# A four-layer network on one core: transposes one pair ahead in the mixing stage, and a memory attention with negated, pre-scaled scores

## What is computed

```python
x = x + tanh(g_ffn[1])   * mixing(_layernorm(x))               # layer 1, feed-forward
x = x + tanh(g_xattn[2]) * memory_attention(_layernorm(x), ctx, mask)   # layer 2, attention

def mixing(x):                      # eight 256x256 factors, summed beforehand
    return einsum('btd,rde->bte', x, factors) / sqrt(8) + bias

def memory_attention(h, m, mask):
    scores = einsum('bsd,bmd->bsm', h, m) / sqrt(256)
    scores = where(mask, scores, -1e30)
    attn = softmax(scores)          # over the 128 memory rows
    out = einsum('bsm,bmd->bsd', attn, m)
    return where(any(mask), out, 0)
```

## Time and profile before

| | |
|---|---|
| median of three timed runs | 903.51 us (902.8 to 904.79) |
| the profiled execution, its own time | 905.36 us |
| its span, first to last instruction | 903.5 us |
| busy: PE / DVE / ACT / POOL | 762.5 / 589.0 / 420.9 / 341.4 us |
| chain that ended last, by engine | PE 53%, DVE 14%, SPq 9%, ACT 8%, issue 8%, POOL 5%, DMA 3% |
| mean granted TensorE clock | 0.909 of full speed |

### The profile page before, as it was taken

How to read it: one execution, slowest core, us unless ns; L and a number is a source line. 1 busy time by engine, 2 the same in 40 slices (tenths; PEclk the granted TensorE clock), 3 DMA queues, 4 the chain that set the end, 5 groups by cost and what they waited for, 6 DMA issues and landing times.

```text
span 903.5 us, 16057 instructions
## 1 busy us (share of the span) xinstructions
PE 762.5 (84%) x4547; PEld 503.1 (56%) x4555; DVE 589.0 (65%) x1388; ACT 420.9 (47%) x920; POOL 341.4 (38%) x571
## 2 busy tenths in 40 slices
PE   3999896998684289898999968999997889999982
PEld 2455454555342156595788756566666555666641
DVE  5799696778776966874322382688874865444446
ACT  3566464676571013341377557666662233333320
POOL 5000552455347613337367652000020761333320
PEclk9999897999997597957999989899997799999995
DMA  6354309999008890144445362000004222232226
GB/s 207 121 175 126 99 9 301 310 287 312 22 0 323 304 283 1 42 183 143 143 147 152 105 195 86 20 20 21 12 1 140 94 95 77 84 87 86 66 79 215
DMA packets 90507, 116.86 MB, mean 129 GB/s; under 512 B 12421, under 2 KB 81064, under 8 KB 89146
## 3 DMA queue, kind: packets, MB, share of 16 engines
q1 hardware_dynamic: 83658, 99.01, 36.2%
q0 software_dynamic: 6768, 16.86, 5.2%
HBM read 54.90 MB, written 58.43 MB: 125 GB/s over the span
## 4 chain that ended last, share of the span: by engine, by line
PE 53%; DVE 14%; SPq 9%; issue 8%; ACT 8%; POOL 5%; DMA 3%; DVEq 0%; POOLq 0%; ACTq 0%
PE ps L2195 8%; SPq L398 7%; PE ps L2086 5%; PE ps L1770 5%; PE ps L2217 4%; POOL x_rows L601 3%; PE ps L1760 3%; PE ps L2104 3%; ACT work L824 2%; ACT probs_t L830 2%; PE ps L1966 2%; PE ps L2079 2%; PE ps L1806 2%; PE ps L2162 2%; PE ps L2069 2%
## 5 line engine op out<-in xcount | busy, mean ns | idle before, releaser
L830 ACT ACTIVATE probs_t<-ps 128x1024 f32<-128x1024 f32 x64 | 65.6, 1024 | 72.8 <-PE ps L1770 72.8
L1223 DVE TENSOR_REDUCE row_max<-ps 128x8 f32<-128x1024 f32 x64 | 77.5, 1210 | 12.0 <-PE ps L1760 11.8
L1087 ACT ACTIVATE ctx_cols<-ctx_cols 128x256 f32<-128x256 f32 x54 | 22.5, 417 | 124.0 <-DVE ctx_cols L1619 124.0
L1229 DVE TENSOR_TENSOR work<-ps,row_max 128x1024 f32<-128x1024 f32 x64 | 76.9, 1202 | 1.2
L1619 DVE TENSOR_TENSOR ctx_cols<-ps,ctx_rows 128x512 f32<-128x512 f32 x54 | 37.3, 690 | 60.6 <-PE ps L2195 60.5
L1770 PE MATMUL ps<-ident,work 128*128 128x128 f32 x512 | 70.6, 282 | 3.3 <-ACT work L824 2.1
L2195 PE MATMUL ps<-early,xt 128*128 x152 | 71.5, 593 | 0.0
L2217 PE MATMUL ps<-early,ctx_cols 128*128 (+1 forms) x216 | 57.7, 391 | 12.2 <-ACT ctx_cols L1092 12.2
L1770 PEld LDWEIGHTS ps<-ident,work 128*128 128x128 f32 x512 | 57.2, 143 | 18.7 <-ACT work L824 13.2
L642 POOL DMA_INDIRECT y_rows<-ctx_cols,w2d x38 | 37.5, 988 | 78.7 <-DMA y_rows<-ctx_cols,w2d 49.0
L2217 PEld LDWEIGHTS ps<-early,ctx_cols 128*128 128x128 f32 x216 | 41.7, 195 | 41.5 <-issue 23.2
(11 more groups left out here) (328 smaller groups left out, 1895.7 us busy)
## 6 DMA issues: line engine op xcount, KB each, us to landing
x_rows<-pad_row SPq DMA_DIRECT2D x1, 17415.0 KB, 68.5
work<-x_rows SPq DMA_DIRECT2D x77, 129.0 KB, 2.1
x_rows<-pad_row SPq DMA_DIRECT2D x1, 7740.0 KB, 36.0
x_rows<-pad_row SPq DMA_DIRECT2D x1, 7611.0 KB, 93.7
early<-in_w3st SPq DMA_DIRECT2D x8, 512.0 KB, 6.4
work<-y_rows SPq DMA_DIRECT2D x16, 256.0 KB, 2.9
early<-y_rows SPq DMA_DIRECT2D x8, 512.0 KB, 7.4
late<-in_w2u SPq DMA_DIRECT2D x1, 2304.0 KB, 8.7
```

What stands on the lines that cost most here:

```text
L830: act.activation(probs_t[:, :, :], ps[:, 4:6, :], ACT.Copy).then_inc(sem("att.evac"), 1)
L1223: dve.tensor_reduce(row_max[:, u, 8 * c:8 * c + 8], scores(c), AX.X, ALU.max).then_inc(sem("att.max"), 1)
L1229: dve.tensor_tensor(probs[:, u, c, :].rearrange("p (h k) -> p h k", k=P), scores(c), row_max[:, u, 8 * c:8 * c + 8].unsqueeze(2).to_broadc ...
```

## The change

Two edits, independent of each other in the code.

**Mixing.** PE now transposes pair t+2 ahead of the products of pair t (`turn_mix`, `mixing`), the first two pairs before any product. ACT's copies alternate between the two pairs of slots of `xt4`, and its wait for `main3` moves two tiles back. DVE normalises two pairs ahead of the first product and from then on pair t+4 instead of t+2. The hardware loops of the stage are written out on PE and ACT.

**Memory attention.** ACT's copy of the transposed tiles multiplies by -1/16, the mask row has the other sign, so the scores arrive negated and scaled; DVE takes their minimum, which is the bias of the exponential as it stands (its scale is then -1). The two 128x1 products and their semaphores go.

```diff
-            def front_ring(L):
-                def body(t, first, last):
-                    for u in range(2):
-                        act.wait_ge(sem("front.tr"), FRONT[L] + t + u + 1)
-                        wait(act, sem(f"main{L}"), t + u - 1)
-                        act.activation(xt[:, u], bank(TP + u, D).rearrange("p (j n) -> p j n", j=2),
-                                       ACT.Copy).then_inc(sem("front.out"), 1)
-                return body
-
-            tile_pairs(act, front_ring(3))
+            for k in range(NT // 2):
+                for u in range(2):
+                    act.wait_ge(sem("front.tr"), FRONT[3] + 2 * k + u + 1)
+                    wait(act, sem("main3"), 2 * k + u - 3)
+                    act.activation(xt4[k % 2][:, u], bank(TP + u, D).rearrange("p (j n) -> p j n", j=2),
+                                   ACT.Copy).then_inc(sem("front.out"), 1)
...
-                    act.wait_ge(sem("l2.bias"), 2 * k + u + 1)
+                    act.wait_ge(sem("l2.least"), 2 * k + u + 1)
...
-                    act.activation(p_l2[:, u], bank(u, P), ACT.Exp, scale=D ** -0.5, bias=sc_l2[:, u, 1:2],
+                    act.activation(p_l2[:, u], bank(u, P), ACT.Exp, scale=-1.0, bias=sc_l2[:, u, 1:2],
...
-                                   ACT.Copy).then_inc(sem("front.out"), 1)
+                                   ACT.Copy, scale=-(D ** -0.5)).then_inc(sem("front.out"), 1)
...
-                    dve.tensor_scalar(mask_bf, mask_u8[0:1], -1.0, -NEG, ALU.add, ALU.mult).then_inc(sem("mask.add"), 1)
+                    dve.tensor_scalar(mask_bf, mask_u8[0:1], -1.0, NEG, ALU.add, ALU.mult).then_inc(sem("mask.add"), 1)
...
             norm_x(3, 0)
-
-            def mixing(t, first, last):
-                if not last:
-                    norm_x(3, t + 2)
+            norm_x(3, 2)
+            for t in range(0, NT, 2):
+                if t + 4 < NT:
+                    norm_x(3, t + 4)
                 for u in range(2):
                     dve.wait_ge(sem("main3"), t + u + 1)
                     add_gated(3, t + u, bank(4 + u, D), tg[:, 5:6])
...
-            def maxima_l2(k):
+            def minima_l2(k):
                 for u in range(2):
                     dve.wait_ge(sem("main4"), 2 * k + u + 1)
-                    dve.tensor_reduce(sc_l2[:, u, 0:1], bank(u, P), AX.X, ALU.max).then_inc(sem("l2.max"), 1)
-                for u in range(2):
-                    dve.wait_ge(sem("l2.max"), 2 * k + u + 1)
-                    dve.tensor_scalar(sc_l2[:, u, 1:2], sc_l2[:, u, 0:1], -(D ** -0.5), None, ALU.mult
-                                      ).then_inc(sem("l2.bias"), 1)
+                    dve.tensor_reduce(sc_l2[:, u, 1:2], bank(u, P), AX.X, ALU.min).then_inc(sem("l2.least"), 1)
...
-            def mixing(t, first, last):
+            def turn_mix(t):
                 for u in range(2):
                     front(3, t + u, u, lambda u: pe.wait_ge(sem("qf.y"), NT))
+
+            def mixing(t):
                 for u in range(2):
                     pe.wait_ge(sem("front.out"), FRONT[3] + t + u + 1)
                     wait(pe, sem("resid3"), t + u - 1)
                     mm(bank(4 + u, D), ones3[32:35, :], b_mix, start=True, stop=False)
                     for j in range(2):
-                        op = mm(bank(4 + u, D), xt[:, u, j, :], w_mix[:, j, :], start=False, stop=(j == 1))
+                        op = mm(bank(4 + u, D), xt4[t // 2 % 2][:, u, j, :], w_mix[:, j, :], start=False, stop=(j == 1))
                     op.then_inc(sem("main3"), 1)
-            tile_pairs(pe, mixing)
+
+            turn_mix(0)
+            for t in range(0, NT, 2):
+                if t + 2 < NT:
+                    turn_mix(t + 2)
+                mixing(t)
```

More of the change, by code:

```diff
@@ L1427, in mixing @@
                     add_gated(3, t + u, bank(4 + u, D), tg[:, 5:6])
-                if last:
+                if t + 2 == NT:
                     norm_x(4, 0)
                 tile_stats(4, t, sem("resid3"))
-            for t in range(0, NT, 2):
-                mixing(t, t == 0, t == NT - 2)
             def weights_l2(k):
@@ L1465, in _ @@
                 if 1 <= k <= NT // 2:
-                    maxima_l2(k - 1)
+                    minima_l2(k - 1)
                 if k >= 2:
```

## The result

The changed kernel takes 897.9 us, the median of 13 runs (896.55 to 901.96); the kernel before, run beside it, 903.76 (901.82 to 905.98). The ratio is 0.9938, with a 95% interval of 0.9923 to 0.9954: 0.6% faster, 5.6 us by the ratio and 5.9 by the medians. The prediction said 898.6.

What follows compares the result with a forecast made beforehand. The prediction took PE to bound the mixing and DVE the memory attention's full-clock steps. Gains of 3.3 + 1.6 = 4.9 us from 903.5 gave 898.6 us, range 894.8 to 901.9, the forecast's own bounds being 897.2 to 900.3.

Steps and rivals of the forecast that it cites:

- Mixing, 3.3 us (2.4 to 3.8): Forecast gain in the mixing stage from transposing a pair ahead: 3.3 us, bounds 2.4 to 3.8.
- six groups stay between products: 6 x 0.44: Mixing: six groups of four transposes still cost 0.44 us each between products, 2.64 us together.
- The start cost: Mixing start: the second pair's transposes ahead of the first product make it 1.0 us later.
- the 0.5 that was to come back: Mixing start: the delayed first pair's last 1.0 us of work falls into the full clock, returning 0.5 us.
- the 3.8 of the upper end: Mixing at best: 4.30 us gone, less 1.0 for the later start, plus 0.5 back, gives 3.8 us.
- rival 1: Mixing: DVE becomes the bound or PE waits for normalised rows; pair 3.2 us, kernel 901.4 us; chance 0.13.
- rival 2: Mixing: the clock rises one pair later, costing 2.1 us more, kernel 900.7 us; chance 0.05.
- Memory attention, 1.6 us (0.8 to 2.5): Forecast gain in the memory attention, mainly from dropping DVE's scalings: 1.6 us, bounds 0.8 to 2.5.
- The step of 3.45: Memory attention at full clock: DVE's step of 3.65 us loses 0.20 and becomes 3.45.
- the 0.3 us by which PE's turn was to start earlier: Memory attention's low-clock opening: PE's turn starts about 0.3 us earlier because the first exponential is freed sooner; 0 to 0.5.
- rival 3: Memory attention's opening: the clock does not fall, 3.3 us less, kernel 895.3 us; chance 0.12.
- Rivals 4 and 5: 4: attention's low clock lasts longer, 2.75 us per step, chance 0.05; 5: gain lost behind the router, 901.1 us, chance 0.05.

Runs made afterwards that it cites:

- e4: The change plus nine unused 256-column products on PE ahead of the mixing stage, on the second chip; 948.02 us against 950.46 before, ratio 0.9982.
- e1: The kernel before with only the mixing edit, on the second chip; 947.81 us against 950.46, ratio 0.9987.
- e3: The kernel before plus unused filler products in PE's gaps ahead of the memory attention's first two transposes, second chip; 948.49 us against 950.46, ratio 0.9993.
- e2: The kernel before with only the memory attention edit, on the second chip; 949.48 us against 950.46, ratio 0.9983.

## Why the prediction was right, and where its sum was not

**Bound of the two stages.** As predicted: PE in the mixing (no releaser ahead of the bias), DVE in the attention's full-clock steps. These are shown, and so is what each edit does by itself; the total came out right partly by luck, as the sum below says.

**Mixing, 3.3 us (2.4 to 3.8).** At a like clock it gives 2.76 (mixing alone), 2.62 (e4) and 2.64 (the change again): within the bounds, 0.5 to 0.7 less than taken. Three terms were mis-sized, and the largest is "six groups stay between products: 6 x 0.44". The 0.44 was read where transposes follow transposes; from transposes to a bias row it is 0.53 (328.56 to 329.09), so 6 x 0.09 = 0.54 is missing. The start cost 1.16 and not 1.0, since all four of the second pair's transposes (1.05 us, 315.96 to 317.01) stood behind the wait for its rows, and not two of them. And of the 0.5 that was to come back only 0.15 to 0.29 did: the first pair's products take 4.35, 4.23 and 4.37 us in these three traces (314.82 to 319.17 in the change again) instead of 4.52, about 0.3 too little. From the 3.8 of the upper end, 3.8 - 0.54 - 0.16 - 0.3 = 2.8, against the 2.62 to 2.76 measured. The 0.5 took for granted that the clock rises at a fixed moment "whatever stands there". It rose 5.7 to 5.8 us after the first transposes in the kernel before and with the attention edit alone, but 7.1 in the filler kernel, whose start is the same code, and 6.3 to 6.5 in the three traces named. So the moment moves by itself; whether the edit moves it too is not shown. In the profiled run of after none of the 0.5 came back.

**DVE's room (rival 1).** It was enough: a pair of 2.97 has DVE wait for 0.18 us. The rival's 3.2 did not come.

**The clock in the mixing (rival 2).** This happened in the profiled run of after, a rise at 323.9 with the first pair's products all at the low clock, and not in the change run again (319.0) nor in e1 and e4 (321.4, 321.6). So it is not the order of the code that decides, but the run (or the chip: the late one is the only trace of the change on the first). Its price was put at 2.1, for a whole pair at the low clock; between two traces of the same kernel the rise is 2.7 us later, counted from the first bias, and costs 1.24, about half of that. The Trainium skill, TensorE: Matmul & The Clock Gate, Part 4: PE-mode transpose, cited for this rival, says that a transpose doesn't count as busy for the clock in the same way as other work. As far as these traces go they don't contradict it: the four more transposes at the start brought no earlier rise, which came 3.9 to 4.2 us after the first bias in four traces of that start (6.9 in after) and 4.5 to 4.7 where only one group stood ahead of it (5.9 in e3). With 5.9 in one trace of the old start the difference is no proof. If it is real, it is worth about 0.3 us here, and not the pair that the rival made of it.

**Memory attention, 1.6 us (0.8 to 2.5).** With the fall it gives 1.37 (e2) and 1.36 (the change again), without it 36.09 - 34.49 = 1.60 (the filler kernel against after, which differ in the two filled gaps too). The step of 3.45 is 3.44, and the 0.3 us by which PE's turn was to start earlier in the low-clock opening is 1.15 - 0.86 = 0.29.

**The fall (rival 3).** It was given 0.12 and a price of 3.3; the price measured is 3.36 and 3.60. The reason against it, that the gap of 0.92 stays, was right as far as it went: the gap stayed, and the clock held all the same. What was wrong was to take the fall as a fixed answer to the gap. Over the ten traces, six have both gaps unfilled and in five of them the clock fell; four have them filled or bridged, and it fell in none of those. If the gaps made no difference, all five falls would land among the six unfilled traces about once in 40 times (6 of the 252 ways to place five falls in ten traces). So the traces together speak for the gaps as what makes the fall possible. The filler's single trace can't show it, since the change held the clock once with its gaps open. What decides it within one kernel was not found. The two edits are not enough to prevent the fall: the clock fell with each alone, and in two of three traces with both.

**The sum.** At a like clock the edits give 67.97 - 63.97 = 4.0 us where 4.9 was forecast. In the trace of after comes 3.6 from the fall that stayed away, less 1.24 from the late rise: 4.0 + 3.6 - 1.24 = 6.36. That this is the table's sum is no check, since the two prices are differences of the same cuts. The 5.6 to 5.9 us of the runs is thus more than the two edits' own work explains. Ten of the 13 runs of after have a mean clock of 0.911 to 0.917 and take 896.6 to 898.2 us, the three others 0.898 to 0.900 and 899.5 to 902.0, so that the clock goes with some 4 us in the time of one kernel. It is more than the one fall: 0.013 of 897 us is 23 us more at half speed, where a fall lasts 10, and only one of these runs has a trace. One fall of 10.2 us at half speed would take the traced run's 0.913 to about 0.907 (an estimate), and no run lies between 0.900 and 0.911, so in most runs of after the fall seems to have stayed away. How often it comes in the kernel before on the first chip stays open, with one trace, and so does whether the change makes it rarer there. So the forecast was off by only 0.7 us by luck: the edits' work, sized 0.9 us too high, was made up for by a clock event that it had given 0.12. On the third chip, where the trace shows the fall, the ratio 0.9953 is 4.5 us, which is the edits' own 4.0 with little added.

**Rivals 4 and 5.** Neither came in the first pair of traces: no step of the attention is slow in after, and the rise behind the router moved by 6.4 us with the work. That a gain does not reach the end did happen on the second chip, in another way than rival 5 told (the last section).

## What to carry to other kernels

Where a stage's transposes wait for a copy, turning the next pair ahead of the products removes the wait for little: here 2.6 to 2.8 us of 28.5. Look at the seams as well: two idles of PE under 1 us each were followed by a fall of the clock in five of six traces, worth 3.4 to 3.6 us. Carrying the same pipelining across the seam gave 1.95 us for the idles, somewhat less than the edit within the stage, and the fall was absent from all three traces with it; the two together are twice what the edit gave. Price a distance on PE by the same neighbour kinds on both sides, and treat the clock's moments as drawn anew in each run: one trace with and one without an event is no comparison of two kernels until each has been seen at a like clock.

## What was not expected of the hardware

**The same code, another clock.** In two traces of the change, on two chips, the rise in the mixing came 4.2 us after the first bias row in one and 6.9 in the other (319.0 - 314.8, 323.9 - 317.0), and the fall came in one and not in the other, with gaps alike to 0.01 us.

**Gains lost further on.** On the second and the third chip, PE, ACT and DVE stand still behind the router while POOL issues its indirect transfers. Waits from 408 to 441 us in the filler kernel (us in total, times, longest), where "remote" is a releaser that the trace does not place on an engine:

```profile
ACT xn L1011 <- remote: 22.2, 4, 10.9
PEld ps L2100 <- issue: 19.8, 3, 9.3
```

and on the first chip, in after, from 400 to 440, where ACT waits for PE and not for something remote:

```profile
ACT xn L1007 <- PE ps L2083: 27.4, 14, 4.0
DVE xn L1537 <- ACT xn L1007: 21.8, 12, 4.2
```

A single wait of ACT is 4.0 us at the longest on the first chip and 10.9 in the filler kernel; on the third chip, in the change again, waits for a remote releaser reach 10.2. The next stage's transposes start at 467.5 us in the filler kernel and at 467.2 in the attention-only one, although the first had begun the router 3.1 us earlier; so on the second chip 3 us were swallowed. On the first chip they start at 438.9 in after and 445.1 before, and the whole gain passes. Why two chips hold the engines up there is open; no run here was made for it.
